# Strips of a banded product in two column tiles, finer weight pieces, and another order of masks, excess strip and first mix groups

## The chip, the cores and the metric

The kernel runs on one core of a Trainium2 chip. The metric is the device time of one launch in microseconds (us), the median of several runs. The engines are TensorE (PE in the profile; its weight loads are PEld), VectorE (DVE), ScalarE (ACT), GpSimd (POOL) and SyncE (SP, which here only issues DMAs). Each engine runs its own queue in order and waits on semaphores.

## The reference

The input x is 4 x 512 rows of 1024 columns, in f32. Two blocks follow each other, and behind each the layer norm of x plus the block's output is taken.

```python
attn = jnp.einsum('ds,td->st', w1, w2) * sparse_mask     # 1024 x 1024
y = jnp.einsum('bds,st->bdt', x, attn) + b2
x = layernorm(x + gelu(y))                               # exact gelu

mask = norm(x, axis=-1) > 64.0
w_l = dequant_kbit(qweight, lut4, 4)                     # 4 bit planes, table of 16 per row
w_h = dequant_kbit(qweight, lut8, 8)
y = jnp.where(mask[..., None], einsum(x, w_h), einsum(x, w_l)) + bias
x = layernorm(x + y)
```

sparse_mask is 1 on windows of 6 along the diagonal and along two more diagonals 32 and 64 beside it, on both sides. So attn is zero outside a band.

## The kernel before, in words

The features are cut into eight units of 128, and the 2048 rows of x into four groups of 512. x is held with features on the partitions, as `z[:, group, unit, 512]`.

**Strips.** Of the product of w1 and w2 only the band is computed, as one strip for each unit b: 128 rows of attn by 272 columns (the unit's own 128 and 72 on each side; 200 columns for the first and the last unit). A strip sums over eight row blocks d of the weights, in f32, each `strip_row(b, d)` being one matmul (two instructions in the trace, L448). `front_strips` makes units 0 to 3, `back_strips(0)` units 4 and 5, `back_strips(1)` units 6 and 7. The weights arrive in pieces: five front pieces, and for each pair of back units two pieces of four row blocks (L285, L286). SP issues them in one queue with the masks of the band, parts of the packed weights and the first pairs of x; that order is the order in which they land.

**Masks.** `mask_strip(b)` on VectorE (L961, L963, L966) multiplies a strip by its mask into mix_raw. ScalarE rounds it to mix_hi (L714) and VectorE subtracts for mix_lo (L973). x is split in the same way, in pairs of units: x_hi on ScalarE (L727) for pairs 1 and 3, on VectorE (L1016) for pairs 0 and 2; x_lo on VectorE (L1018). A few rows of the band reach further than a strip; `excess_strip` (L442) computes them from gathered weights into unit 4's bank, `make_mix_e` (L987 to L999) masks them, and `make_xe_lo` (L1006) makes the matching x.

**Mix.** For each group g, TensorE runs `own(g, t)` (unit t with itself, three matmuls of 512 columns, L481 to L483), `beside(g, t)` (units t and t + 1 with each other, in two row tiles, L506 and L508) and `excess(g, pair)` (L493) into one bank per unit. In group 0 the excess strip stands behind own(0,1), and turn(0) behind own(0,7). ScalarE takes each finished unit through `gelu` (L735), which also frees the bank for the next group. own(g, t) waits for gelu of the group before and for x_lo of its pair; own(1,0) and own(1,1) wait for lin_lo(0) too.

**Decode.** Beside all this, ScalarE and VectorE expand the packed 4-bit weights, block by block (eight blocks), in numbered steps of 11 to a block: a leaf on ScalarE (L753), a merge on VectorE (L1045), two half blocks of planes on VectorE (L1030), a sum of rows and a centring on ScalarE (L758, L763) with the mean between them on VectorE (L1049), and the addition of the identity (L1057). Written lists say how many steps each engine runs at which place: `EARLY_STEPS[b]` ahead of mask b, `MIX_STEPS[g]` in group g (the first number behind gelu(g, 0) and ahead of xe_hi(g + 1), the second further on), `FIRST_STEPS` and `SECOND_STEPS` behind the mix. `turn(b)` on TensorE turns a decoded block, `make_lin_hi` and `make_lin_lo` split it.

**Behind the mix** TensorE multiplies x with the decoded weights, three matmuls of up to 512 columns for each block (L577 to L579), until the end.

Of the kernel before, what the change touches and what calls it, by code (L numbers as in the profile page):

```python
# [38 lines left out]
def post_ln_block(nc, xt, xr, xe_in, w1d, w1e, w2d, w2e, b2c, mask, mask_b, mask_e, mask_rest, qbits, lut4, lut8, bias, out):  # L39
# [26 lines left out]
    HALF_BLOCKS = KB // 2  # L66
    QUARTER = D // 4
# [33 lines left out]
    with ctx:  # L101
# [106 lines left out]
        def by_word(row):  # L208
            return row.rearrange("p (s w k) -> p k s w", s=BITS, k=KB)

        w_loaded = [sem(f"w_loaded{n}") for n in range(len(ROW_PIECES) + 4)]
# [10 lines left out]
        warm_made, consts_made, flips_made = (sem(n) for n in ("warm_made", "consts", "flips"))  # L222
# [7 lines left out]
        ones_made, g_ones_made = sem("ones_made"), sem("g_ones_made")  # L230
# [19 lines left out]
        (g_table_loaded, g_table_step, g_decoded, g_rows_summed, g_row_mean, g_centred, g_w_ready, g_turned, g_lin_hi_made,  # L250
         g_lin_lo,
         g_low_rows, g_bits_made, g_compared, g_blended) = (
             sem(f"g_{n}") for n in ("table", "table_step", "decoded", "rows_summed", "row_mean", "centred", "w_ready", "turned",
# [7 lines left out]

        def places_of(b):
            first, end = strip_of(b)
            return slice(first - b * P + REACH, end - b * P + REACH)
# [7 lines left out]
        def _(sp):  # L272
# [8 lines left out]
            def load_back(n, h):  # L281
                signal = w_loaded[len(ROW_PIECES) + 2 * n + h]
                rows = slice(h * HALF_BLOCKS, (h + 1) * HALF_BLOCKS)
# [148 lines left out]
        def _(pe):  # L432
# [222 lines left out]
            with nc.tensor.If(wanted > 0):  # L655
# [40 lines left out]
                pe.wait_ge(g_ones_made, 1)  # L696
# [6 lines left out]
        def _(act):  # L703
# [37 lines left out]
            def make_leaf(b, i):  # L741
                if i == 0:
# [3 lines left out]
                    if b == 0:  # L746
                        act.wait_ge(flips_made, 1)
# [143 lines left out]
            with nc.scalar.If(wanted > 0):  # L891
# [29 lines left out]
                def general_weights(blocks_before, steps_before, steps):  # L921
                    for h in range(2):
                        with act.Fori(0, HALF_BLOCKS) as c:
# [28 lines left out]
        def _(dve):  # L952
# [56 lines left out]
            def make_x_lo(g, r):  # L1009
                if r in X_ON_ACT:  # L1010
                    dve.wait_ge(x_hi_made, len(X_ON_ACT) * g + X_ON_ACT.index(r) + 1)
                else:
# [4 lines left out]
                    dve.wait_ge(x_rounded, (PAIRS - len(X_ON_ACT)) * g + r // 2 + 1)  # L1017
# [72 lines left out]
            def make_flips():  # L1090
# [11 lines left out]
                                        ALU.subtract).then_inc(flips_made, 1)  # L1102
# [236 lines left out]
            with nc.vector.If(wanted > 0):  # L1339
# [63 lines left out]
                def general_weights(bits, blocks_before, steps_before):  # L1403
                    steps, leaves = table_steps(bits), 2 ** bits
                    for half in range(2):
                        with dve.Fori(0, HALF_BLOCKS) as c:
# [34 lines left out]
                            dve.wait_ge(g_centred, c + (before + 1))  # L1441
# [29 lines left out]
        def _(pool):  # L1471
# [85 lines left out]
            with nc.gpsimd.If(wanted > 0):  # L1557
# [6 lines left out]
                nc.gpsimd.memset(g_ones[:, :].bitcast(f32), 1.0).then_inc(g_ones_made, 1)  # L1564
# [114 lines left out]
```

## Time and profile before

| | |
|---|---|
| median of 3 runs | 296.92 us (295.55 to 296.94) |
| profiled execution | 297.11 us, span 295.1 us |
| TensorE busy | 280.9 us, 95% of the span |
| VectorE busy | 222.3 us, 75% |
| ScalarE busy | 196.1 us, 66% |
| DMA, 7 to 36 us | 374 GB/s |

The span is the time from the first to the last instruction of the profiled execution. Busy shares are means over stages that have different limits; what a hole in one engine costs is read from who waits for it.

### The profile page before, as it was taken

To read this page: it belongs to the slowest core of one execution; us is meant where nothing else is said; L and a number is where in the kernel's file an instruction comes from. 1 tells how busy PE (TensorE), PEld (TensorE's weight loads), DVE (VectorE), ACT (ScalarE), POOL (GpSimd) and SP (SyncE) were. 2 spreads that over 40 slices of the span, in tenths; PEclk is the share of its full clock that TensorE was granted. 3 is DMA by queue.
4 is the path that set the end of the run, shared out by engine and by line. 5 is a ranking of instruction groups with operands and counts; after the bars stand their busy time and mean duration, and the time that the engine had idled before them with its cause. 6 is when DMAs were issued, how large, how long until landed. Compare 5 with 4: busy or idle time off the path is not lost.

```text
span 295.1 us, 4871 instructions
## 1 busy us (share of the span) xinstructions
PE 280.9 (95%) x1835; PEld 245.2 (83%) x1835; DVE 222.3 (75%) x380; ACT 196.1 (66%) x257; POOL 57.0 (19%) x83
## 2 busy tenths in 40 slices
PE   6999999899999999999999999999999999999990
PEld 2788866667668999999999999999988887887780
DVE  1679999897868977997979686297589778656272
ACT  2866368988999879989989996472457484113110
POOL 4000001533354211221200000001141124262101
PEclk9999999999999999999999999999999999999998
DMA  6999999999999711111111111165088754333423
GB/s 207 400 359 359 376 376 340 242 244 244 207 201 195 147 39 36 56 36 51 40 39 53 38 53 38 51 141 221 16 289 273 244 196 178 113 139 117 171 92 132
DMA packets 28480, 49.78 MB, mean 169 GB/s; under 512 B 2464, under 2 KB 11936, under 8 KB 28448
## 3 DMA queue, kind: packets, MB, share of 16 engines
q1 hardware_dynamic: 23392, 40.53, 39.9%
q0 software_dynamic: 4352, 8.39, 15.8%
q10 hardware_dynamic: 704, 0.46, 0.5%
q8 instruction: 17, 0.28, 0.4%
q14 instruction: 15, 0.12, 0.1%
HBM read 36.79 MB, written 12.58 MB: 167 GB/s over the span
## 4 chain that ended last, share of the span: by engine, by line
PE 69%; ACT 7%; SPq 7%; DVE 7%; issue 5%; DMA 3%; POOLq 0%; POOL 0%; DVEq 0%; ACTq 0%
PE acc L577 17%; PE acc L579 17%; PE acc L578 17%; PE acc L506 4%; DMA w<-in_w2d 3%; PE acc L481 2%; SPq L286 2%; ACT leaf L753 2%; ACT zz L796 2%; PE acc L516 2%; PE acc L482 2%; PE acc L483 2%; DVE leaf L1045 1%; PE acc L560 1%; DVE zz L1087 1%
## 5 line engine op out<-in xcount | busy, mean ns | idle before, releaser
L577 PE MATMUL acc<-lin,zz 128*128 128x256 f32 (+2 forms) x424 | 130.7, 308 | 0.3 <-issue 0.3
L579 PE MATMUL acc<-lin,zz 128*128 128x256 f32 (+2 forms) x424 | 129.9, 306 | 0.0
L578 PE MATMUL acc<-lin,zz 128*128 128x256 f32 (+2 forms) x424 | 129.5, 305 | 0.0
L577 PEld LDWEIGHTS acc<-lin,zz 128*128 128x128 f32 x424 | 80.1, 189 | 4.5 <-issue 0.5
L579 PEld LDWEIGHTS acc<-lin,zz 128*128 128x128 f32 x424 | 80.0, 189 | 4.1
L578 PEld LDWEIGHTS acc<-lin,zz 128*128 128x128 f32 x424 | 80.2, 189 | 3.9
L753 ACT ACTIVATE leaf<-planes,lut,flip 128x1024 f32<-128x1024 uint8 x56 | 67.5, 1237 | 1.3 <-DVE dest L1045 1.3
L1045 DVE COPY_PREDICATED leaf<-planes,leaf 128x1024 f32<-128x1024 uint8 x32 | 43.6, 1364 | 13.9 <-ACT leaf L753 13.2
L864 ACT ACTIVATE junk<-rows,cols 128x1024 bf16<-128x1024 f32 x15 | 17.2, 1147 | 34.1 <-DVE cols L1171 34.1
L1045 DVE COPY_PREDICATED dest<-planes,leaf 128x1024 f32<-128x1024 uint8 x24 | 32.5, 1356 | 3.7 <-ACT leaf L753 2.3
L1533 POOL DMA_DIRECT2D z<-in_xr x16 | 19.4, 1218 | 70.9 <-ACT z L735 69.5
L448 PE MATMUL acc<-w,w 128*128 128x272 f32 (+1 forms) x128 | 28.2, 380 | 2.1 <-DMA w<-in_w2d 2.1
L448 PEld LDWEIGHTS acc<-w,w 128*128 128x128 f32 x128 | 23.5, 190 | 7.4 <-DMA w<-in_w2d 3.8
L1165 DVE SCALAR_TENSOR_TENSOR rows<-acc,cols,bias_bc 128x512 f32<-128x512 f32 x15 | 11.3, 750 | 18.4 <-PE acc L579 18.3
L1087 DVE TENSOR_TENSOR zz<-z,zz 128x1024 fp32r<-128x1024 f32 x16 | 19.3, 1220 | 7.6 <-ACT zz L796 7.6
L735 ACT ACTIVATE z<-acc,b 128x512 f32<-128x512 f32 x32 | 20.4, 692 | 4.2 <-PE acc L508 4.2
L846 ACT ACTIVATE parts<-acc 128x258 f32<-128x258 f32 (+1 forms) x32 | 12.1, 379 | 12.8 <-PE acc L579 12.7
L1018 DVE TENSOR_TENSOR x_lo<-z,x_hi 128x1024 fp32r<-128x1024 f32 x16 | 19.0, 1223 | 0.3
L1507 POOL TENSOR_TENSOR cols<-cols 128x4 f32<-128x4 f32 x4 | 5.4, 1352 | 70.3 <-DVE cols L1195 70.3
L1501 POOL TENSOR_SCALAR cols<-parts 128x1 f32<-128x1 f32 x16 | 9.8, 612 | 41.4 <-ACT parts L846 41.4
L796 ACT ACTIVATE zz<-z 128x1024 fp32r<-128x1024 f32 x16 | 16.6, 1064 | 0.0
L851 ACT ACTIVATE off_band<-off_band 128x896 f32<-128x896 f32 x8 | 7.6, 953 | 12.2 <-DMA off_band<-in_mask_rest 12.2
(115 smaller groups left out, 408.4 us busy)
## 6 DMA issues: line engine op xcount, KB each, us to landing
z<-in_xt SPq DMA_DIRECT2D x16, 512.0 KB, 8.7
z<-in_xr POOLq DMA_DIRECT2D x16, 512.0 KB, 8.5
out_rows<-rows SPq DMA_DIRECT2D x15, 512.0 KB, 3.4
out_rows<-parts SPq DMA_DIRECT2D x32, 128.0 KB, 1.7
rows<-out_rows SPq DMA_DIRECT2D x16, 256.0 KB, 2.8
w<-in_w1d SPq DMA_DIRECT2D x7, 512.0 KB, 9.0
off_band<-in_mask_rest SPq DMA_DIRECT2D x8, 448.0 KB, 4.8
w<-in_w2d SPq DMA_DIRECT2D x3, 584.0 KB, 9.0
```

Source lines behind the costliest of these rows:

```text
L448: return nc.tensor.matmul(unit_bank(b)[:, places_of(b)], w1[:, d, b * P:(b + 1) * P], w2[:, d, first:end], start=d == 0, stop=d == KB - 1)
L577: nc.tensor.matmul(bank, hi, w_hi, start=k == 0, stop=False)
L578: nc.tensor.matmul(bank, hi, w_lo, start=False, stop=False)
L579: last = nc.tensor.matmul(bank, lo, w_hi, start=False, stop=k == KB - 1)
L735: nc.scalar.activation(z[:, g, t, :], unit_bank(t), ACT.Gelu, bias=b2[:, t:t + 1]).then_inc(gelu_done, 1)
L753: nc.scalar.activation(to, planes[:, b % 2, 0, :], ACT.Identity, bias=lut[:, b, 2 * i:2 * i + 1], scale=flip[:, b, i:i + 1]).then_inc(leaf ...
L796: nc.scalar.activation(zz[:, 1, g, 2 * r:2 * r + 2, :], z[:, g, 2 * r:2 * r + 2, :], ACT.Copy).then_inc(z_hi_made, 1)
L864: nc.scalar.activation(junk[:, :], rows[:, j % 4, :], ACT.Square, bias=neg_mean2[:, j:j + 1], accum_out=sq2[:, j:j + 1]).then_inc(squared2, 1)
L1018: nc.vector.tensor_tensor(x_lo[:, 2 * r:2 * r + 2, :], z[:, g, 2 * r:2 * r + 2, :], x_hi[:, 2 * r:2 * r + 2, :].bitcast(f32), ALU.subtract ...
L1045: nc.vector.copy_predicated(to, planes[:, b % 2, plane, :], leaf[:, other, :]).then_inc(merged, 1)
L1087: nc.vector.tensor_tensor(zz[:, 0, g, 2 * r:2 * r + 2, :], z[:, g, 2 * r:2 * r + 2, :], zz[:, 1, g, 2 * r:2 * r + 2, :].bitcast(f32), ALU. ...
L1533: nc.gpsimd.dma_start(z[:, g, 2 * r:2 * r + 2, :], xr[g, 2 * r:2 * r + 2].rearrange("k p n -> p k n"), accum_op=ALU.add).then_inc(residual ...
```

## The change

Five things. (1) Each strip row becomes two matmuls: the first 64 rows of the unit with the columns to its left and its own, the last 64 rows with its own and those to its right; each has 64 stationary columns and at most 200 moving ones and writes its own half of the partitions. (2) The back weights come in pieces of two row blocks, four for each pair of units. (3) The excess strip moves behind own(0,3). In group 0 x_hi of pair 0 is made on ScalarE too; mask 6 comes ahead of x_lo(0,1), and mix_hi 6 ahead of x_hi(0,1). (4) In every group beside(g,2) moves ahead of excess(g,0) and beside(g,0); group 1 runs its first four units in the order 2, 3, 0, 1; lin_hi(0) comes behind gelu(0,2). (5) The decode steps are spread anew: 15 instead of 17 early, 5, 4, 4 and 2 in the groups instead of 6, 3, 3 and 2, and one more in the fourth tile behind the mix. The rest joins semaphores of one engine, most of them in a branch that isn't taken with these inputs.

```diff
+    BACK_ROWS = 2
+    BACK_PIECES = KB // BACK_ROWS
...
-    X_ON_ACT = (1, 3)
+    X_ON_ACT = ((0, 1, 3),) + ((1, 3),) * (GROUPS - 1)
...
-    EARLY_STEPS = [11, 1, 1, 1, 1, 2, 0, 0]
-    MIX_STEPS = [(3, 3), (2, 1), (2, 1), (2, 0)]
+    EARLY_STEPS = [13, 1, 1, 0, 0, 0, 0, 0]
+    MIX_STEPS = [(4, 1), (3, 1), (4, 0), (2, 0)]
...
-    FIRST_STEPS = [2, 2, 2, 1, 1, 2, 1, 2, 1, 2, 2, 2, 2, 2, 2, 2]
+    FIRST_STEPS = [2, 2, 2, 2, 1, 2, 1, 2, 1, 2, 2, 2, 2, 2, 2, 2]
...
-    BESIDE = (0, 2, 1, 3, 5, 4, 6)
+    BESIDE = (2, 0, 1, 3, 5, 4, 6)
+    OWN_OF_TURN = (2, 3, 0, 1)
...
             load_back(0, 0)
+            load_back(0, 1)
             load_band(0)
+            load_back(0, 2)
+            load_back(0, 3)
             load_q(1)
-            load_back(0, 1)
             load_back(1, 0)
+            load_back(1, 1)
             load_band(1)
             load_x(0, 0)
-            load_back(1, 1)
+            load_back(1, 2)
+            load_back(1, 3)
             load_x(0, 1)
...
             def strip_row(b, d):
-                first, end = strip_of(b)
-                return nc.tensor.matmul(unit_bank(b)[:, places_of(b)], w1[:, d, b * P:(b + 1) * P], w2[:, d, first:end],
-                                        start=d == 0, stop=d == KB - 1)
+                for rows_, low, high in ((slice(0, SIDE), REACH, 0), (slice(SIDE, P), 0, REACH)):
+                    first, end = max(b * P - low, 0), min((b + 1) * P + high, D)
+                    to = unit_bank(b)[rows_, first - b * P + REACH:end - b * P + REACH]
+                    half = w1[:, d, b * P + rows_.start:b * P + rows_.stop]
+                    last = nc.tensor.matmul(to, half, w2[:, d, first:end], start=d == 0, stop=d == KB - 1)
+                return last
...
             for g in range(GROUPS):
-                for t in range(4):
+                for t in OWN_OF_TURN if g == FIRST_TURN_GROUP + 1 else range(4):
                     own(g, t)
-                    if (g, t) == (0, 1):
+                    if (g, t) == (0, 3):
                         excess_strip()
+                beside(g, 2)
                 excess(g, 0)
                 beside(g, 0)
-                beside(g, 2)
...
                 if b == KB - 1:
-                    make_x_hi(0, 1)
+                    make_x_hi(0, 0)
                 if b:
                     make_mix_hi(b - 1)
+                if b == KB - 1:
+                    make_x_hi(0, 1)
...
                 gelu(g, 1)
                 if g + 1 < GROUPS:
                     make_x_hi(g + 1, 1)
+                gelu(g, 2)
                 if g == FIRST_TURN_GROUP:
                     make_lin_hi(0)
-                gelu(g, 2)
                 gelu(g, 3)
...
                 if b == KB - 2:
                     make_x_lo(0, 0)
+                if b == KB - 1:
                     make_x_lo(0, 1)
                 mask_strip(b)
```

## Rows read from the trace of the kernel before

**Rows 1.** view of stretches; after the length: busy us (and instructions) of each engine, granted clock, DMA
```profile
36.00:63.00 27.00, 24.72 (x152) 17.97 (x151) 24.98 (x37) 20.99 (x27) 5.85 (x7) 1.00 1.04 308
63.00:92.00 29.00, 28.86 (x176) 20.29 (x175) 22.46 (x29) 27.42 (x38) 12.25 (x11) 1.00 1.12 220
92.00:290.00 198.00, 194.79 (x1374) 181.66 (x1372) 149.82 (x252) 126.53 (x170) 35.83 (x54) 1.00 0.35 113
```

**Rows 2.** page, 40 slices: granted clock in tenths
```profile
PEclk9999999999999999999999999999999999999998
```

**Rows 3.** chain of waits, in order of time: start, us, what
```profile
22.22 9.96 DMA w<-in_w2d
32.22 3.45 PE acc L448 x16
```

**Rows 4.** timeline of TensorE: start, us, engine, line, what, idle before
```profile
35.37 0.53 PE L481 MATMUL acc<-x_hi,mix_hi 128*128 128x512 f32 x1
...
36.88 1.88 PE L442 MATMUL acc<-w_e 128*128 128x48 f32 x16
...
41.03 0.39 PE L506 MATMUL acc<-x_hi,mix_hi 64*128 64x512 f32 x1
41.03 0.39 PE L508 MATMUL acc<-x_hi,mix_hi 64*128 64x512 f32 x1
...
44.45 0.47 PE L481 MATMUL acc<-x_hi,mix_hi 128*128 128x512 f32 x1 [0.18 <-DVE x_lo L1018]
...
52.39 0.47 PE L481 MATMUL acc<-x_hi,mix_hi 128*128 128x512 f32 x1 [0.92 <-ACT z L735]
...
57.83 0.47 PE L481 MATMUL acc<-x_hi,mix_hi 128*128 128x512 f32 x1 [0.64 <-DVE x_lo L1018]
```

**Rows 5.** timeline of VectorE, to group 1
```profile
32.05 0.38 DVE L961 TENSOR_TENSOR mix_raw<-acc,band 128x128 f32<-128x128 f32 x1
...
38.80 0.26 DVE L987 TENSOR_TENSOR raw_e<-acc,band_e 128x96 f32<-128x96 f32 x1 [0.42 <-PE acc L442]
...
44.23 1.34 DVE L1045 COPY_PREDICATED dest<-planes,leaf 128x1024 f32<-128x1024 uint8 x1
...
47.40 0.75 DVE L1006 SCALAR_TENSOR_TENSOR xe<-xe_raw,cols,xe 128x512 fp32r<-128x512 f32 x1 [0.28 <-ACT xe L721]
...
48.79 2.36 DVE L1018 TENSOR_TENSOR x_lo<-z,x_hi 128x1024 fp32r<-128x1024 f32 x2
...
68.95 0.63 DVE L1030 TENSOR_SCALAR planes<-q_low 128x256 uint16<-128x256 uint16 x4
```

**Rows 6.** timeline of ScalarE, end of the masks
```profile
32.88 0.42 ACT L714 ACTIVATE mix_hi<-mix_raw 128x256 fp32r<-128x256 f32 x1 [0.61 <-DVE mix_raw L966]
33.49 1.06 ACT L727 ACTIVATE x_hi<-z 128x1024 fp32r<-128x1024 f32 x1 [0.20 <-DMA z<-in_xt]
```

**Rows 7.** timeline of TensorE, groups 2 and 3
```profile
65.31 0.50 PE L481 MATMUL acc<-x_hi,mix_hi 128*128 128x512 f32 x1
...
77.57 0.50 PE L481 MATMUL acc<-x_hi,mix_hi 128*128 128x512 f32 x1
...
82.36 0.50 PE L481 MATMUL acc<-x_hi,mix_hi 128*128 128x512 f32 x1
```

**Rows 8.** timeline of ScalarE, start of group 2
```profile
69.52 0.69 ACT L735 ACTIVATE z<-acc,b 128x512 f32<-128x512 f32 x1 [0.59 <-PE acc L508]
70.11 1.23 ACT L753 ACTIVATE leaf<-planes,lut,flip 128x1024 f32<-128x1024 uint8 x1
71.24 1.14 ACT L763 ACTIVATE dest<-dest,cols 128x1024 f32<-128x1024 f32 x1
72.29 0.61 ACT L721 ACTIVATE xe<-xe_raw 128x512 fp32r<-128x512 f32 x1
```

**Rows 9.** timeline of VectorE, x_lo of group 3
```profile
74.43 2.36 DVE L1018 TENSOR_TENSOR x_lo<-z,x_hi 128x1024 fp32r<-128x1024 f32 x2
...
80.58 2.40 DVE L1018 TENSOR_TENSOR x_lo<-z,x_hi 128x1024 fp32r<-128x1024 f32 x2
```

More of the change, by code:

```diff
@@ L1 @@
+import itertools
 import numpy as np
@@ L81, in post_ln_block @@
     LATE = (LAST_PAIR, LAST_PAIR + 1)
-    X_ON_ACT = (1, 3)
+    X_ON_ACT = ((0, 1, 3),) + ((1, 3),) * (GROUPS - 1)
+    X_HI_BEFORE = list(itertools.accumulate((len(pairs) for pairs in X_ON_ACT), initial=0))
+    X_ROUNDED_BEFORE = [PAIRS * g - n for g, n in enumerate(X_HI_BEFORE)]
     DECODE = LEAVES + 3
-    EARLY_STEPS = [11, 1, 1, 1, 1, 2, 0, 0]
-    MIX_STEPS = [(3, 3), (2, 1), (2, 1), (2, 0)]
+    EARLY_STEPS = [13, 1, 1, 0, 0, 0, 0, 0]
+    MIX_STEPS = [(4, 1), (3, 1), (4, 0), (2, 0)]
     MIX_Z = {2: ((0, 0), (0, 1)), 3: ((0, 2), (0, 3))}
     FIRST_Z = [((1, 0), (1, 1)), ((1, 2),), ((1, 3),)] + [((2 + n // PAIRS, n % PAIRS),) for n in range(2 * PAIRS)] + [()] * 5
-    FIRST_STEPS = [2, 2, 2, 1, 1, 2, 1, 2, 1, 2, 2, 2, 2, 2, 2, 2]
+    FIRST_STEPS = [2, 2, 2, 2, 1, 2, 1, 2, 1, 2, 2, 2, 2, 2, 2, 2]
     SECOND_STEPS = [3, 2, 2, 3, 2, 2, 2, 3, 2, 2, 2, 3, 2, 2, 2, 3]
-    BESIDE = (0, 2, 1, 3, 5, 4, 6)
+    BESIDE = (2, 0, 1, 3, 5, 4, 6)
     HALVES = 2 * len(BESIDE)
     FIRST_TURN_GROUP = 0
+    OWN_OF_TURN = (2, 3, 0, 1)
     TURN_IN_FIRST = {6: 2, 12: 3}
@@ L209, in by_word @@
             return row.rearrange("p (s w k) -> p k s w", s=BITS, k=KB)
-        w_loaded = [sem(f"w_loaded{n}") for n in range(len(ROW_PIECES) + 4)]
+        w_loaded = [sem(f"w_loaded{n}") for n in range(len(ROW_PIECES) + 2 * BACK_PIECES)]
         band_loaded = [sem(f"band_loaded{s}") for s in range(2)]
@@ L221, in post_ln_block @@
         residual_done = [sem(f"residual_done{r}") for r in range(PAIRS)]
-        warm_made, consts_made, flips_made = (sem(n) for n in ("warm_made", "consts", "flips"))
+        warm_made, consts_made = sem("warm_made"), sem("consts")
         planes_made, leaf_made, merged = sem("planes_made"), sem("leaf_made"), sem("merged")
@@ L249, in post_ln_block @@
                                      "x_loaded", "x_hi", "x_lo", "mixed", "gelu", "residual"))
-        (g_table_loaded, g_table_step, g_decoded, g_rows_summed, g_row_mean, g_centred, g_w_ready, g_turned, g_lin_hi_made,
+        (g_table_loaded, g_table_step, g_decoded, g_w_ready, g_turned, g_lin_hi_made,
          g_lin_lo,
          g_low_rows, g_bits_made, g_compared, g_blended) = (
-             sem(f"g_{n}") for n in ("table", "table_step", "decoded", "rows_summed", "row_mean", "centred", "w_ready", "turned",
+             sem(f"g_{n}") for n in ("table", "table_step", "decoded", "w_ready", "turned",
                                      "lin_hi", "lin_lo", "low_rows", "bits", "compared", "blended"))
@@ L260, in strip_of @@
             return max(b * P - REACH, 0), min((b + 1) * P + REACH, D)
-        def places_of(b):
-            first, end = strip_of(b)
-            return slice(first - b * P + REACH, end - b * P + REACH)
         def blocks_of(b):
@@ L281, in load_back @@
             def load_back(n, h):
-                signal = w_loaded[len(ROW_PIECES) + 2 * n + h]
-                rows = slice(h * HALF_BLOCKS, (h + 1) * HALF_BLOCKS)
+                signal = w_loaded[len(ROW_PIECES) + BACK_PIECES * n + h]
+                rows = slice(h * BACK_ROWS, (h + 1) * BACK_ROWS)
                 part, cut = slice(HALF + n * QUARTER, HALF + (n + 1) * QUARTER), slice(turn_of[n], turn_of[n + 1])
@@ L926, in general_weights @@
                             nc.scalar.activation(dest[:, 0, :], dest[:, 0, :], ACT.Copy,
-                                                 accum_out=row_sum[:, 0:1]).then_inc(g_rows_summed, 1)
-                            act.wait_ge(g_row_mean, c + (before + 1))
+                                                 accum_out=row_sum[:, 0:1]).then_inc(rows_summed, 1)
+                            act.wait_ge(row_mean_made, c + (KB + before + 1))
                             nc.scalar.activation(dest[:, 0, :], dest[:, 0, :], ACT.Identity,
-                                                 bias=neg_row_mean[:, 0:1]).then_inc(g_centred, 1)
+                                                 bias=neg_row_mean[:, 0:1]).then_inc(centred, 1)
                             act.wait_ge(g_turned, c + (before + 1))
@@ L1016, in make_x_lo @@
                     nc.vector.tensor_copy(x_hi[:, 2 * r:2 * r + 2, :], z[:, g, 2 * r:2 * r + 2, :]).then_inc(x_rounded, 1)
-                    dve.wait_ge(x_rounded, (PAIRS - len(X_ON_ACT)) * g + r // 2 + 1)
+                    dve.wait_ge(x_rounded, X_ROUNDED_BEFORE[g] + [n for n in range(PAIRS) if n not in X_ON_ACT[g]].index(r) + 1)
                 nc.vector.tensor_tensor(x_lo[:, 2 * r:2 * r + 2, :], z[:, g, 2 * r:2 * r + 2, :],
@@ L1440, in general_weights @@
                                     g_decoded, 1)
-                            dve.wait_ge(g_centred, c + (before + 1))
+                            dve.wait_ge(centred, c + (KB + before + 1))
                             block_ = by_word(dest[:, 0, :])[:, bass.ds(c + HALF_BLOCKS * half, 1), :, :].rearrange(
```

23 lines of the change are left out of this document (11 added, 12 removed).

## The prediction

> **What bounds the kernel now.** I read the stretches first: from 36 to 63 us TensorE is busy 24.72 of 27 us, from 63 to 92 us 28.86 of 29, from 92 to 290 us 194.79 of 198 [rows 1]. So from 63 us on the kernel is a TensorE queue without holes (the holes at the very end are the tail). A microsecond that TensorE wins or loses before 63 us is worth a microsecond at the end, and the only holes that could be won are the 2.3 us between 36 and 63. The granted clock is 1.00 in these stretches [rows 1] and nine tenths or more in all slices but the last [rows 2]: the level of 2.4 GHz. The chain of waits shows what sets the start of the mix: the last weight piece, issued at 22.22, lands at 32.18, and sixteen matmuls follow it [rows 3]. TensorE's timeline shows the rest of the start: own(0,0) at 35.37, the excess strip at 36.88, own(0,6) at 44.45, own(1,0) at 52.39 after 0.92 us idle, own(1,4) at 57.83 after 0.64 us idle for x_lo [rows 4].
>
> **The strips.** The sixteen matmuls behind the last piece are four rows of 272 columns and four of 200, two instructions to a row, in 3.45 us with a tail of about 0.3 us [rows 3]: 0.227 and 0.167 us an instruction, in proportion to the columns, so 0.453 us for a wide row and 0.333 for a narrow one. After the change each row is two halves of 200 moving columns or fewer, and 64 stationary columns. No row of before shows column tiles. If the halves run together, a row costs 0.333 us; if one follows the other, 0.667. Two neighbours: matmuls of two row tiles both start at 41.03 us and both last 0.39 us, so they share their time [rows 4], which speaks for the lower end; the excess strip, with 48 moving columns, takes 1.88 us for sixteen instructions [rows 4], 0.107 for a load and a matmul, and two such pairs for each pass would make 0.43 a row. I take 0.333, because the row pairs are the nearest row, and keep 0.43 and 0.667 for the range.
>
> The Trainium skill, "TensorEngine Tiling (Array Packing)", Key Properties, says that different tiles can load weights and multiply in parallel. By that rule a row would cost what I take; no run here shows it for column tiles. The same list says that a change of the tiling mode drains the engine, which speaks against the change; the strips change mode once, at their end, and the sum would be the same to about a tail.
>
> The weights' bytes and their place ahead of the last piece don't change: the same pieces are halved, and the first x pair and both bands stay ahead of the last one. So it lands at 32.2 as before. Behind it stand two rows of two units instead of four: unit 6 is done after three rows, at 32.2 + 1.0 + about 0.25 = 33.45, unit 7 at 33.8, where the strips now end at 35.67. That is the whole gain of tiles and pieces, 1.9 us; earlier gains only lengthen the waits for the next piece.
>
> **What the masks now hold back.** On VectorE the queue is x_lo(0,0), mask 6, mix_lo 4, x_lo(0,1), mask 7. On ScalarE it is x_hi(0,0), mix_hi 6, x_hi(0,1). Earlier masks are out of the way: mask 5 stands at 32.05 now, in a VectorE that never waits from 21 us on [rows 5]; 15 instead of 17 decode steps lie ahead of it, a merge of 1.34 us and half a block of planes (0.54) less, so it can start by 30.2. With 0.83 for the mask, 0.41 for mix_hi 5, 1.06 for x_hi(0,0) and 1.2 for x_lo(0,0) that pair is made by 33.7 at the latest, and by about 33 if the band's wait of before shrinks. Mask 6 then waits for unit 6: 33.5. A mask takes 0.83 us to its release of mix_hi (32.05 to 32.88) [rows 5, 6], so mix_hi 6 starts at 34.33, takes 0.41, and x_hi(0,1), whose data landed at 33.49, runs from 34.75 for 1.06 us [rows 6]. x_lo(0,1) follows with 1.2 us to 37.05, and own(0,2) starts at 37.2. TensorE has finished own(0,0) and own(0,1) by 35.2: the strips' gain ends in a wait of 2 us.
>
> The excess strip now stands behind own(0,3). From own(0,0) to the excess strip two units took 1.51 us [rows 4]; so it starts at 38.7 in place of 36.88, 1.8 us later, and VectorE, which is in order, starts raw_e at 40.6 instead of 38.80 [rows 5]. Everything behind it in that queue (xe_lo, x_lo(0,2), mix_lo 6 and 7, x_lo(0,3)) keeps its lengths, so own(0,6) starts at 46.25 instead of 44.45. Beside(0,2), moved ahead of excess(0,0), runs in the wait for mix_e and gains nothing, since own(0,4) and own(0,6) wait for x_lo.
>
> **Group 0's decode.** VectorE's first step of the mix moves from 44.23 [rows 5] to 46.05. It is now half a block of planes, about 0.54 us of the 0.63 that one takes [rows 5] since neighbours overlap, and then the mean of block 0. ScalarE's centre waits for this mean until 46.75; behind it in ScalarE's queue stand two leaves, then xe_hi(1): 1.05 + 1.13 + 1.13 + 0.61 (the lengths are those of [rows 8]), so xe_hi(1) ends at 50.7. From the start of xe_lo to the end of the second x_lo it is 3.75 us (47.40 to 48.79 + 2.36) [rows 5], which gives 54.45 and, with 0.15 to TensorE, 54.6. Own(1,2), the first of the new order, needs exactly that x_lo(1,1). Without waits TensorE would be there at 46.25 + 7.0 = 53.25. So group 1 starts at 54.6 against 52.39: +2.2. Starting with units 2 and 3 hides lin_lo(0), which ends 1.15 us behind x_lo(1,1), and with one merge less before x_lo(1,2) the 0.64 us wait at 57.83 goes: -0.6. Group 1's leaves, merges, xe_lo and x_lo(2,0) end 12.2 us after its start, against the 12.26 that a group takes (65.31 to 77.57) [rows 7]: no wait, by a hair. Group 2 starts +1.6 us late.
>
> **Group 2's four steps.** This term doesn't depend on what came before. Now gelu(2,0) starts 4.21 us after own(2,0) (69.52, 65.31), then ScalarE runs a leaf and a centre before xe_hi(3) at 72.29; x_lo(3,0) ends at 74.43 + 1.2 and own(3,0) starts at 77.57 [rows 7 to 9], so it has 1.8 us to spare. Two things eat them. Beside(2,2) and the excess stand ahead of beside(2,0), on whose end gelu(2,0) waits: +0.7 (three passes of 0.23). And four steps come before xe_hi(3) where there were two: one leaf and one sum of rows more, 1.13 + 1.05 = +2.2 [rows 8]. 1.8 - 0.7 - 2.2 = -1.1: group 3 starts 1.1 us late against group 2. In the same way z_hi(0,0), z_lo and x_lo(3,2) come 1.9 us later; x_lo(3,2) ends at 80.58 + 1.2 and own(3,4) starts at 82.36 [rows 7, 9], with 0.4 us to spare behind the 0.15, and the stall gives 1.1 more: 0.4 + 1.1 - 1.9 = -0.4.
>
> **The sum.** 2.2 - 0.6 + 1.1 + 0.4 = +3.1 us on the profiled execution's 297.11, that is 300.2. Its median stands 0.2 below the profiled one, so I forecast 300.0. The decode step moved into the first tiles' turn (a leaf and a merge) goes into idle time of ScalarE or adds up to 0.6 us at the third turn; it stays in the range. Two more edits cost nothing: the joined semaphores, and more DMA issues on SP, which now runs some 9 us ahead of the landings (22.22 against 32.18); that cover gone, four pairs of issues would cost a few us.
>
> **Rivals.** (a) Faster: TensorE alone limits groups 0 and 1. Speaks for it: strips end 1.9 us earlier, a group needs 12.26 us, and the new order takes both named waits out. Groups 0 and 1 from 33.8 with 1.7 us for the excess strip and 1.0 for the turn put group 2 at 61.0 against 65.31, -4.3, and with group 2's +1.5 the time is 294.3. It decides at x_lo(0,1): it would have to be made by 35.2 us, not 37.05. Against it: the orders of both queues. (b) No change that can be told: the decode queues catch up half, group 1 starts less than 0.7 us late: 296 to 298.4. (c) Column tiles one after the other: 5.1 us for each of eight row steps, 6.4 + 40.8, unit 6 near 47 instead of 33.45, +13.5 on top: 313.7. At 0.43 us a row unit 6 is about 1 us later: 301. (d) The clock falls to 1.2 GHz in the new gap of about 2.5 us ahead of the last two pieces. The rows show 1.00 through the waits of before [rows 2], so little speaks for it; the last rows and units would cost twice, some +3: 303.
>
> The Trainium skill, "TensorE: Matmul & The Clock Gate", Part 3, gives 2.38 times for three column tiles of narrow bf16 matmuls. An estimate from that page would put two tiles close to together, so a row near 0.4 us and the result at that of the 0.43 case; nothing here shows it yet.
>
> **How the numbers follow.** Forecast, with 0.333 to 0.43 a row and the uncertainty of each wait (298.4 to 302): 0.64. (a) 0.13, (b) 0.13, (c) with true serial tiles 0.06, (d) 0.04. The range goes from the middle of (b) to (d), 296.9 to 303, and leaves out (a), (c) and a part of (b) and (d). About 0.5% is what a measurement of this kernel can tell from no change: 295.4 to 298.4 is "same". Faster is (a), 0.13; same is (b), 0.13; slower is the rest, 0.74.
>
> **What would show it.** Right: strip halves that start in pairs; unit 7 done near 33.8; own(0,2) idle before it until 37.2, released by x_lo; raw_e near 40.6; own(1,2) near 54.6; own(3,0) idle about 1 us before it. Wrong at once: own(0,2) right behind own(0,1), a last piece that lands much before 32, or own(3,0) without idle time.

## The result, and the profile after

The changed kernel takes 301.11 us (median, 300.32 to 302.02) against 296.63 us of the kernel before: a ratio of 1.0137, with a 95% interval of 1.0112 to 1.0161. Timed again in the run after5 it gave 1.0112 (1.0083 to 1.0141). It is slower: by 4.1 us by the ratio (1.37% of 296.63), by 4.5 us by the two medians; 300.0 was forecast, in a range of 296.9 to 303.0. The profiled execution took 302.02 us with a span of 300.2 us, 5.1 us more than the span before.

First the chain of waits of the changed kernel, in order of time (start, us, what), from the third piece of the last weights to group 1:

```profile
23.77 7.44 DMA w<-in_w2d
31.25 4.29 PE acc L458 x25
...
35.64 0.37 DVE mix_raw L973
...
36.46 0.42 ACT mix_hi L724
36.88 0.96 ACT x_hi L737
...
37.86 1.24 DVE x_lo L1030
...
39.23 0.47 PE acc L491
...
40.84 1.73 PE acc L449 x16
...
42.59 0.27 DVE raw_e L999
...
48.10 0.55 DVE planes L1042 x4
48.65 0.07 DVE cols L1061
...
48.75 1.15 ACT dest L773
49.90 1.18 ACT leaf L763 x2
...
52.07 0.62 ACT xe L731
...
55.25 1.23 DVE x_lo L1030
...
56.62 0.47 PE acc L491
```

It is the chain of the forecast: mask 6 (L973) releases mix_hi 6 (L724), behind it x_hi(0,1) (L737), x_lo(0,1) (L1030), two units of the mix and the excess strip (L449), raw_e (L999); then x_lo(0,3), a plane step, the mean (L1061), the centre (L773), two leaves (L763), xe_hi(1) (L731), and on VectorE the split of x's first two pairs for group 1. What differs from the forecast is its start, 2.1 us late (mask 6 at 35.64 instead of 33.5). TensorE's timeline (the last bracket is the idle time before the instruction and what ended it) has the same places as [rows 4, 7]:

```profile
31.25 4.60 PE L458 MATMUL acc<-w,w 128*64 128x200 f32 x32 [2.10 <-DMA w<-in_w2d]
...
39.23 0.47 PE L491 MATMUL acc<-x_hi,mix_hi 128*128 128x512 f32 x1 [1.78 <-DVE x_lo L1030]
...
40.68 1.88 PE L449 MATMUL acc<-w_e 128*128 128x48 f32 x16
...
48.25 0.47 PE L491 MATMUL acc<-x_hi,mix_hi 128*128 128x512 f32 x1 [0.18 <-DVE x_lo L1030]
...
56.62 0.47 PE L491 MATMUL acc<-x_hi,mix_hi 128*128 128x512 f32 x1 [0.25 <-DVE x_lo L1030]
```

The same timeline from group 2 to own(3,4):

```profile
68.88 0.50 PE L491 MATMUL acc<-x_hi,mix_hi 128*128 128x512 f32 x1
...
82.13 0.47 PE L491 MATMUL acc<-x_hi,mix_hi 128*128 128x512 f32 x1 [0.92 <-ACT z L745]
...
87.40 0.47 PE L491 MATMUL acc<-x_hi,mix_hi 128*128 128x512 f32 x1 [0.47 <-DVE x_lo L1030]
```

| start of, us | before | after | later by |
|---|---|---|---|
| excess strip | 36.88 | 40.68 | 3.8 |
| own(0,6) | 44.45 | 48.25 | 3.8 |
| group 1 | 52.39 | 56.62 | 4.2 |
| group 2 | 65.31 | 68.88 | 3.6 |
| group 3 | 77.57 | 82.13 | 4.6 |
| own(3,4) | 82.36 | 87.40 | 5.0 |

From there on TensorE is nearly without holes, and the 5.0 us arrive at the end. The view of stretches shows it against [rows 1]: the loss is TensorE's idle time between 36 and 63 us, now 4.8 us instead of 2.3, and 1.4 us between 63 and 92, where there was 0.1. In the columns, the figure ahead of the last two is the granted clock:

```profile
36.00:63.00 27.00, 22.16 (x129) 15.77 (x129) 20.77 (x36) 18.48 (x24) 5.17 (x6) 1.00 0.83 265
63.00:92.00 29.00, 27.62 (x168) 19.18 (x166) 24.85 (x32) 26.52 (x36) 10.49 (x9) 1.00 1.12 227
92.00:290.00 198.00, 196.95 (x1385) 182.69 (x1384) 149.20 (x246) 131.89 (x177) 37.48 (x55) 1.00 0.37 113
```

The same view in short stretches, from the strips' last pieces on, with the clock again ahead of the last two figures:

```profile
28.00:29.00 1.00, 1.00 (x14) 0.72 (x10) 0.90 (x4) 0.42 (x1) 0.00 (x0) 1.00 1.12 352
...
30.00:31.00 1.00, 0.00 (x0) 0.00 (x0) 0.95 (x4) 0.40 (x2) 0.00 (x0) 1.00 1.16 358
...
32.00:33.00 1.00, 1.00 (x11) 1.00 (x9) 1.00 (x1) 0.00 (x0) 0.00 (x0) 0.50 1.01 391
...
34.00:35.00 1.00, 1.00 (x10) 0.75 (x9) 0.00 (x0) 0.00 (x0) 0.00 (x0) 0.50 1.05 383
...
36.00:37.00 1.00, 1.00 (x5) 0.82 (x5) 0.84 (x4) 0.54 (x2) 0.00 (x0) 1.00 1.04 379
```

This is what the forecast had only as its rival (d): TensorE has no work from 29.2 to 31.25 us, and soon after the clock stands at 0.50, the level of 1.2 GHz, for over three microseconds. The last thirty-two strip instructions took 4.60 us; at full clock (a_x, below) they take 3.03.

### The profile page after: what moved, and what is told of

The parts are those of the page before. It is cut to its first block, busy times and chain, and to the rows that moved or that the text cites. A ratio compares the mean times of both kernels' runs of the same rounds, so it can differ in the third digit from the quotient of the medians.

```text
span 300.2 us, 5135 instructions
## 1 busy us (share of the span) xinstructions
PE 278.3 (93%) x1963; PEld 242.5 (81%) x1963; DVE 221.4 (74%) x379; ACT 196.3 (65%) x258; POOL 57.2 (19%) x83
## 4 chain that ended last, share of the span: by engine, by line
PE 63%; ACT 10%; DVE 9%; SPq 7%; issue 6%; DMA 2%; POOLq 0%; POOL 0%; ACTq 0%; DVEq 0%
PE acc L587 17%; PE acc L589 16%; PE acc L588 16%; ACT leaf L763 3%; DMA w<-in_w2d 2%; DVE x_lo L1030 2%; SPq L288 2%; ACT zz L806 2%; SPq L289 2%; DVE zz L1099 2%; PE acc L516 2%; PE acc L491 2%; PE acc L526 2%; PE acc L458 1%; PE acc L570 1%
## 5 line engine op out<-in xcount | busy, mean ns | idle before, releaser
L763 ACT ACTIVATE leaf<-planes,lut,flip 128x1024 f32<-128x1024 uint8 x56 | 67.4, 1237 | 1.2 <-DVE dest L1057 0.7
L1546 POOL DMA_DIRECT2D z<-in_xr x16 | 20.2, 1265 | 75.1 <-ACT z L745 70.5
L458 PE MATMUL acc<-w,w 128*64 128x200 f32 (+1 forms) x256 | 25.1, 346 | 5.8 <-DMA w<-in_w2d 5.8
L458 PEld LDWEIGHTS acc<-w,w 128*64 128x64 f32 x256 | 21.0, 144 | 10.1 <-DMA w<-in_w2d 9.0
L1030 DVE TENSOR_TENSOR x_lo<-z,x_hi 128x1024 fp32r<-128x1024 f32 x16 | 19.1, 1223 | 2.2 <-ACT x_hi L737 1.9
L491 PE MATMUL acc<-x_hi,mix_hi 128*128 128x512 f32 x32 | 13.9, 433 | 4.4 <-DVE x_lo L1030 3.4
L1514 POOL TENSOR_SCALAR cols<-parts 128x1 f32<-128x1 f32 x16 | 9.1, 571 | 42.4 <-ACT parts L858 42.4
```

Source lines behind the costliest of these rows:

```text
L458: last = nc.tensor.matmul(to, half, w2[:, d, first:end], start=d == 0, stop=d == KB - 1)
L491: nc.tensor.matmul(bank, hi, x_hi[:, t, :], start=True, stop=False)
L763: nc.scalar.activation(to, planes[:, b % 2, 0, :], ACT.Identity, bias=lut[:, b, 2 * i:2 * i + 1], scale=flip[:, b, i:i + 1]).then_inc(leaf ...
L1030: nc.vector.tensor_tensor(x_lo[:, 2 * r:2 * r + 2, :], z[:, g, 2 * r:2 * r + 2, :], x_hi[:, 2 * r:2 * r + 2, :].bitcast(f32), ALU.subtract ...
L1546: nc.gpsimd.dma_start(z[:, g, 2 * r:2 * r + 2, :], xr[g, 2 * r:2 * r + 2].rearrange("k p n -> p k n"), accum_op=ALU.add).then_inc(residual ...
```

## The experiments

Each run's ratio is to the kernel before on the same chip, with its 95% interval. "Milestones" are starts in the profiled execution, so they are good to some tenths of a microsecond, while the timed runs of one kernel spread over 1 to 3.6 us. A difference of two ratios is shown only where it is larger than their intervals.

**Keep TensorE at work in the wait (a_fill).**

```diff
+                    if n == 1 and d == 2 * BACK_ROWS:
+                        for _ in range(20):
+                            nc.tensor.matmul(unit_bank(KB - 1)[:, 288:512], warm[:, 0:P], warm[:, 0:224], start=False, stop=False)
```

> The changed kernel with twenty bf16 matmuls of 224 columns put into TensorE's wait ahead of the third back piece of units 6 and 7; they write columns that no one reads. Theory (the fallen clock makes the strips late, and each microsecond of strips reaches the end through mask 6, x_hi(0,1) and x_lo(0,1)): the granted clock stays at 1.00, unit 7's strip ends near 34.2 instead of 35.7, own(0,2) starts near 37.7 instead of 39.2, and the time is 299.4 to 300.2. Rival (the end of the strips doesn't matter, the queues behind it do): the strips end earlier, own(0,2) stays at 39.2 and the time at 301.1.

1.0128 (1.0074 to 1.0183), 300.84 us. TensorE's timeline of this run, with the filling matmuls and the last strip instructions:

```profile
29.10 2.09 PE L475 MATMUL acc<-warm 128*128 128x224 bf16 x20
31.23 3.07 PE L458 MATMUL acc<-w,w 128*64 128x200 f32 x32
```

And from own(0,2) to group 1:

```profile
37.69 0.60 PE L494 MATMUL acc<-x_hi,mix_hi 128*128 128x512 f32 x1 [1.80 <-DVE x_lo L1033]
...
40.22 2.39 PE L449 MATMUL acc<-w_e 128*128 128x48 f32 x16
...
56.66 0.47 PE L494 MATMUL acc<-x_hi,mix_hi 128*128 128x512 f32 x1 [0.28 <-DVE x_lo L1033]
```

The first half came as expected. The strips end at 34.3 and own(0,2) starts at 37.69, so the strips' end does set it, and the rival falls. But no time is won: the wait for x_lo(0,1) is still 1.80 us, and now the clock falls there. It stood at 0.50 from 37.9 to 41.3 us; the excess strip took 2.39 us instead of 1.88, raw_e starts at 42.65 as without the filling (42.59), and group 1 at 56.66. The clock fell once more, from 44.7 to 48.1 us. That one cost the chain nothing: from own(0,4) to group 1 it is 10.16 us, and 10.17 in the changed kernel, whose clock was full there.

**One matmul a row again (a_wide).**

```diff
-                for rows_, low, high in ((slice(0, SIDE), REACH, 0), (slice(SIDE, P), 0, REACH)):
-                    ...
+                first, end = strip_of(b)
+                to = unit_bank(b)[:, first - b * P + REACH:end - b * P + REACH]
+                return nc.tensor.matmul(to, w1[:, d, b * P:(b + 1) * P], w2[:, d, first:end], start=d == 0, stop=d == KB - 1)
```

> The changed kernel with each strip row again as one matmul of up to 272 columns; two-row pieces and all orders stay. Theory (two column tiles only turn strip time into waits for the weights, and let the clock fall): TensorE has no hole over 1 us before the last piece, the clock stays at 1.00, the strips end near 34.9, own(0,2) starts near 38.4, and the time is 300.5 to 301.3, not worse than with the tiles. Rival (the tiles' shorter rows are a gain of their own): the strips end 0.5 us or more later than 35.7 and the time is 301.8 to 303.

1.0178 (1.0135 to 1.022), 302.15 us; the profiled execution took 301.62. TensorE's timeline of this run, the strips and then own(0,2):

```profile
10.82 24.25 PE L456 MATMUL acc<-w,w 128*128 128x200 f32 x112 [0.85 <-DMA w<-in_w2d]
...
38.44 0.47 PE L488 MATMUL acc<-x_hi,mix_hi 128*128 128x512 f32 x1 [1.98 <-DVE x_lo L1027]
```

The profile has what the theory said: the strips run without a hole, the clock stays at 1.00 past the mix, the strips end at 35.07, own(0,2) starts at 38.44 and group 1 at 55.83, 0.8 us earlier than in the changed kernel's profile. So up to the mix the tiles are no gain when the clock falls in the strips; when it holds (a_fill, a_x), their strips end at 34.3, 0.8 us ahead of a_wide's. The timed runs don't show these 0.8 us: the interval overlaps that of the changed kernel and lies, if anything, above it, though in the profile most of the lead is still there at the last turn (200.36 against 201.02). Why stays open.

**x's second pair ahead of mask 6 (a_x).**

```diff
                 if b == KB - 1:
                     make_x_hi(0, 0)
+                    make_x_hi(0, 1)
                 if b:
                     make_mix_hi(b - 1)
-                if b == KB - 1:
-                    make_x_hi(0, 1)
...
                     make_x_lo(0, 0)
-                if b == KB - 1:
                     make_x_lo(0, 1)
```

> The changed kernel with x_hi(0,1) ahead of mix_hi 6 on ScalarE and x_lo(0,1) ahead of mask 6 on VectorE. Theory (mask 6 ahead of x's second pair costs TensorE a wait of 1.8 us ahead of own(0,2) and so moves the excess strip): own(0,2) follows own(0,1) without idle time, raw_e starts near 40.6 instead of 42.6, group 1 near 54.6, and the time is 2 us less than the changed kernel's, 298.7 to 299.5. Rival (mask 6 and 7 come later and their mix_lo hold back own(0,4) to own(0,6) just as much): 300.6 to 301.4.

1.0076 (1.0046 to 1.0105), 299.60 us: 1.5 to 1.8 us won against the changed kernel, just short of the 2 us expected. The wait ahead of own(0,2) is 0.51 us instead of none, the excess strip starts at 37.83 instead of 40.68, group 1 at 53.77. That is 2.85 us in the profile, of which 1.6 are the strips' end at 34.26 with the clock at 1.00. In this execution it fell only at 43.9 us, which again cost the chain nothing: the last turn comes 2.80 us earlier, too. What the order alone is worth is read against a_g2 (below), which has the changed kernel's order up to group 2 and nearly the same history of the clock: the excess strip starts 1.36 us earlier here (37.83 against 39.19), group 1 1.35 us (53.77 against 55.12). TensorE's timeline of this run at own(0,2):

```profile
36.37 0.47 PE L491 MATMUL acc<-x_hi,mix_hi 128*128 128x512 f32 x1 [0.51 <-DVE x_lo L1029]
```

**And the excess strip behind own(0,1) (a_x_exc).**

```diff
-                    if (g, t) == (0, 3):
+                    if (g, t) == (0, 1):
```

> The changed kernel with x's second pair ahead of mask 6 (as in the run before with that edit alone) and the excess strip back behind own(0,1). Theory (raw_e and all behind it on VectorE wait for the excess strip): raw_e starts near 38.4 instead of 39.75 of that run, group 1 1.3 us earlier, and the time is 1.0 to 1.5 us less than with x's pair alone, a ratio to the kernel before of 1.002 to 1.005. Rival (mask 7 and mix_lo 5 to 7 set raw_e or own(0,4) by then): the same ratio as with x's pair alone, 1.0076.

1.0045 (1.0024 to 1.0065), 298.55 us, another 0.9 us in the ratio, inside what was expected; the interval overlaps that of a_x, so by time alone the step isn't shown. The profile has it: group 1 starts at 52.94, 0.8 us earlier than in a_x, although the clock fell again behind the wait ahead of the last pieces and the strips ended 1.3 us later, at 35.58.

**Two of group 2's steps moved to group 3 (a_g2).**

```diff
-    MIX_STEPS = [(4, 1), (3, 1), (4, 0), (2, 0)]
+    MIX_STEPS = [(4, 1), (3, 1), (2, 0), (4, 0)]
```

> The changed kernel with two of group 2's four decode steps moved to group 3: MIX_STEPS of (4,1), (3,1), (2,0), (4,0). Theory (the leaf and the sum of rows ahead of xe_hi(3) make group 3 late, whatever came before): own(3,0) starts 12.3 us after own(2,0) instead of 13.25 and own(3,4) 4.8 us after own(3,0) instead of 5.3, 1.4 us won; group 3's longer list then delays z_hi and z_lo of the pairs that the first squares wait for, by up to 1.3 us, so the time falls by 0 to 1.2 us against the changed kernel. Rival (group 3 waits for something that these steps don't move): own(3,0) stays 13.2 us behind own(2,0).

Group 3 starts 12.29 us after group 2 (79.64, 67.35), and own(3,4) 4.78 us after that: the mechanism is as it was read. No time is won, 1.0164 (1.0119 to 1.021), where 0 to 1.2 us were expected: the steps in group 3 now keep z_lo back, and the first squares wait for it, as TensorE's timeline of this run shows:

```profile
94.80 2.17 PE L570 MATMUL acc<-zz 128*128 128x256 f32 x16 [1.72 <-DVE zz L1099]
```

Up to group 2 this is the changed kernel, and in its profile the clock held until about 43 us. So it shows that kernel's start of the mix at full clock. TensorE's timeline has the excess strip, VectorE's has mask 6:

```profile
39.19 1.88 PE L449 MATMUL acc<-w_e 128*128 128x48 f32 x16
```

```profile
34.13 0.38 DVE L973 TENSOR_TENSOR mix_raw<-acc,band 128x128 f32<-128x128 f32 x1 [0.72 <-PE acc L458]
```

**The same two steps taken to the place ahead of mask 6 (a_early).**

```diff
-    EARLY_STEPS = [13, 1, 1, 0, 0, 0, 0, 0]
-    MIX_STEPS = [(4, 1), (3, 1), (4, 0), (2, 0)]
+    EARLY_STEPS = [13, 1, 1, 0, 0, 0, 2, 0]
+    MIX_STEPS = [(4, 1), (3, 1), (2, 0), (2, 0)]
```

> The changed kernel with two of group 2's steps taken to the place ahead of mask 6, where VectorE waits: EARLY_STEPS of 13, 1, 1, 0, 0, 0, 2, 0 and MIX_STEPS of (4,1), (3,1), (2,0), (2,0). Theory (the mean of block 0 first in group 0 keeps ScalarE's centre, xe_hi(1) and group 1 waiting; two steps too many do the same in group 2): own(0,2) stays where it is, xe_hi(1) comes 1.1 us earlier against own(0,6), group 3 starts 12.3 us after group 2, and the time is 2.0 to 2.8 us less than the changed kernel's. Rival (the steps ahead of mask 6 delay x_lo(0,0) and mask 6 by what they save later): no gain beyond 0.5 us.

1.0121 (1.0088 to 1.0153), 300.80 us: the timed runs can't tell it from the changed kernel (1.0137 and 1.0112), and the expected 2.0 to 2.8 us were too much. In the profile the later parts come as expected: group 3 follows group 2 by 12.24 us, without a wait behind it, and nothing waits at the squares. From own(0,6) to group 1 it is 7.97 us instead of 8.37, 0.4 us won where 1.1 was expected: the leaf behind the second one needs a merged buffer, and ScalarE waits for VectorE's merge. But the rival is right in part. The clock held in this execution, and the strips ended at 34.28, yet mask 6 starts only at 35.39, as VectorE's timeline shows:

```profile
34.14 1.23 DVE L1030 TENSOR_TENSOR x_lo<-z,x_hi 128x1024 fp32r<-128x1024 f32 x1 [1.22 <-ACT x_hi L737]
35.39 0.38 DVE L973 TENSOR_TENSOR mix_raw<-acc,band 128x128 f32<-128x128 f32 x1
```

The two steps keep x_hi(0,0) on ScalarE back to 33.06 (30.93 in the changed kernel), and with it x_lo(0,0) and mask 6. Against a_g2, whose strips end at 34.34, mask 6 and the excess strip are 1.3 us late (35.39 against 34.13, 40.46 against 39.19). So at full clock these steps cost 1.3 us ahead of the mix, of some 1.9 us that they win behind it (0.4, 1.0 and 0.5 at groups 1 and 3 and own(3,4)). In the changed kernel's own profile, with the fallen clock, VectorE waits 2.42 us ahead of mask 6, so there was room for them.

**All three orders undone (a_sum).** The edits of a_x, a_x_exc and a_early together.

> The changed kernel with its three order parts undone together: x's second pair ahead of mask 6, the excess strip behind own(0,1), and the step lists of 13, 1, 1, 0, 0, 0, 2, 0 and (4,1), (3,1), (2,0), (2,0). Tiles, two-row pieces, beside(g,2) first and group 1's new order stay. Theory (the orders explain the loss; their parts add up): group 1 starts near 52.5, group 3 near 77.1, the ratio to the kernel before is 0.998 to 1.003. Rival (tiles and pieces cost by themselves, through the clock or late landings): 1.005 or more.

0.9974 (0.9957 to 0.9992), 296.66 us, just below the expected range. The orders were the loss: undone together they win 1.4% against the changed kernel timed beside it (1.0112) and end a little below the kernel before, with the tiles still there and the clock still falling for three microseconds ahead of the strips' end. Group 1 starts at 53.41 and group 3 at 77.93, 0.9 and 0.8 us later than expected. One by one the edits gave 0.61%, 0.31% and 0.16% in the ratios, 1.1% in all, each with some 0.3% to either side, so they add up to the 1.4% no better than within that; the last two aren't shown singly by the times.

**Only tiles and two-row pieces (b_tiles), only tiles (b_tiles4).** The kernel before with the change's strip_row and loads, every order as before; and with strip_row alone.

```diff
-                return nc.tensor.matmul(to, w1[:, d, b * P:(b + 1) * P], w2[:, d, first:end], start=d == 0, stop=d == KB - 1)
+                for rows_, low, high in ((slice(0, SIDE), REACH, 0), (slice(SIDE, P), 0, REACH)):
+                    ...
```

> The kernel before with only the two column tiles and the two-row pieces; every order and every list of steps as before. Theory (in the old order VectorE's two x_lo and masks 6 and 7, not the strips, set the start of raw_e): raw_e stays within 0.5 us of 38.8 and the time is that of before, 296.1 to 297.1. Rival (the shorter strips reach the end): own(0,0) near 34, raw_e near 37.2 and 294.8 to 295.4.

> The kernel before with the two column tiles alone; the weights in four-row pieces as before. Theory (in the run with two-row pieces in the old order it was band 0, landing 1 us late behind more and smaller transfers, that moved the masks): the first mask starts at 20.5 again, raw_e within 0.3 us of 38.8, the ratio is 0.999 to 1.001 as long as the clock holds; if it falls in the wait of some 2.5 us ahead of the last piece, eight rows at half the clock end the strips near 37.5 and the ratio is 1.004 to 1.007. Rival (the tiles, not the pieces, moved the masks): the first mask starts near 21.5 again.

b_tiles: 1.0052 (1.003 to 1.0075), 298.36 us; b_tiles4: 1.001 (0.9988 to 1.0032), 297.46 us. Neither theory holds; in b_tiles4 the rival does (the tiles, not the pieces, moved the masks). In both, the tiles win nothing: the strips end at 35.8 and 35.5 us (35.67 before), and the first mask starts at 21.5 and 21.4 us, where the kernel before has 20.5 and the two profiles of the next kernel, which has no tiles, 21.07 (b_own) and 20.40 (b_own5). VectorE waits for the band's mask to land (L964 and L962 are the mask's line in either kernel). VectorE's timeline at that mask, first of b_tiles4:

```profile
21.43 0.39 DVE L964 TENSOR_TENSOR mix_raw<-acc,band 128x128 f32<-128x128 f32 x1 [1.48 <-DMA band<-in_mask_b]
```

And of b_own5, which has no tiles:

```profile
20.40 0.38 DVE L962 TENSOR_TENSOR mix_raw<-acc,band 128x128 f32<-128x128 f32 x1 [0.85 <-DMA band<-in_mask_b]
```

Everything behind is late by this: raw_e starts at 39.71 and 39.73 instead of 38.80 (39.35 and 38.60 in b_own and b_own5). Part of this is spread: in b_own the landings up to the first band are 0.6 us later than in the kernel before, in b_tiles4 0.4 us already at the last front piece. Counted from there, the first band transfer lands after 4.0 us in the profiles without tiles and after 4.5 in b_tiles4, 5.3 in b_tiles. The pieces alone are not the cause, since b_tiles4 has four-row pieces and a_wide, with two-row pieces, has 4.0; nor is the clock, which never fell in b_tiles4 up to the mix's end. What differs is the width of the strips' matmuls. A clean pair are the changed kernel and a_wide, which issue the same band transfer at the same 11.6 us; the time to its landing follows, first in the changed kernel, with tiles:

```profile
L293 SPq DMA_DIRECT2D band<-in_mask_b x1: 1387/1387/1387, 11.6 to 11.6; - x1
...
DMA to landing us min/median/max: 9.8/9.8/9.8
```

And in a_wide, without them:

```profile
L293 SPq DMA_DIRECT2D band<-in_mask_b x1: 1378/1378/1378, 11.6 to 11.6; - x1
...
DMA to landing us min/median/max: 9.0/9.0/9.0
```

**Only group 1's new order (b_own, b_own5).** The kernel before with the parts of the change that act on group 1.

```diff
-    MIX_STEPS = [(3, 3), (2, 1), (2, 1), (2, 0)]
+    MIX_STEPS = [(3, 2), (2, 2), (2, 1), (2, 0)]
+    OWN_OF_TURN = (2, 3, 0, 1)
...
-                for t in range(4):
+                for t in OWN_OF_TURN if g == FIRST_TURN_GROUP + 1 else range(4):
...
+                gelu(g, 2)
                 if g == FIRST_TURN_GROUP:
                     make_lin_hi(0)
-                gelu(g, 2)
```

> The kernel before with only group 1's order 2, 3, 0, 1, lin_hi(0) behind gelu(0,2), and one step moved from group 0 to group 1: MIX_STEPS of (3,2), (2,2), (2,1), (2,0). Theory (the parts of the change that take waits out of group 1 are a gain when nothing else is moved): the 0.92 us wait ahead of group 1 and the 0.64 us ahead of own(1,4) go, group 2 starts 1.0 to 1.5 us earlier than 65.3, and the ratio to the kernel before is 0.994 to 0.997. Rival (the waits only move, to x_lo of group 1 or 2): 1.000.

> The kernel of b_own again, to have its interval: the kernel before with group 1's order 2, 3, 0, 1, lin_hi(0) behind gelu(0,2), and one step moved from group 0 to group 1. By its first run: a ratio of 0.992 to 0.995, and no wait of TensorE on VectorE or ScalarE between 46 us and the end of the mix. A rival (its first run had a lucky clock): 0.997 to 1.000.

0.9931 (0.9907 to 0.9955) and 0.9936 (0.992 to 0.9952), 295.05 and 295.56 us: faster than both kernels. The edit is three things at once (the order of units, lin_hi(0), one step moved from group 0 to group 1); they were not tried apart. The waits of TensorE between 46 and 92 us are gone from the list of who waited for whom; what is left is issue time behind the mix. The view of TensorE's waits of b_own5, 46 to 92 us:

```profile
PE acc L578 <- issue: 0.3, 1, 0.3
```

Group 2 starts 19.24 us after own(0,6) (63.50, 44.26) where it was 20.86 [rows 4, 7]: 1.6 us, the 0.92 and the 0.64 of the two waits.

**The changed kernel again (after5).**

> The changed kernel itself, on the same chip as the others of this call: by its record a ratio of 1.011 to 1.016 to the kernel before, own(0,2) behind a wait of 1.8 us for x_lo, and group 3 13.25 us behind group 2; the clock falls for some 3 us in one of the waits between 28 and 43 us, not always in the same.

1.0112 (1.0083 to 1.0141). The wait ahead of own(0,2) is 1.79 us, group 3 follows group 2 by 13.27 us. The clock fell twice, from 31.0 to 34.4 us and from 44.7 to 48.1 us; from own(0,4) to group 1 it is 10.17 us all the same.

The budget from the ratios: group 1's new order -0.67% (mean of b_own and b_own5), tiles and two-row pieces +0.52% (b_tiles), the three orders +1.38% (1.0112 against 0.9974). Together +1.23%, where the changed kernel measured +1.37% and +1.12%. The last term is itself taken from the 1.0112, so what the sum really tests is a_sum: the first two terms give -0.15%, and it measured -0.26% (-0.43 to -0.08). x_hi of pair 0 on ScalarE, beside(g,2) first and the step added behind the mix stay in a_sum and were not tried alone.

## Why the prediction was right

The forecast of 3.1 us came as 4.1 by the ratio, 4.5 by the medians and 5.1 in the spans of the profiled executions. The delays behind the strips came by the steps it named and in nearly their sizes; what is too small in the sum is the strips' term, and it alone accounts for the difference in the profile: own(0,6) is 2.0 us later than forecast, group 1 2.0, own(3,4) still 1.9.

- **The strips.** Column tiles do run together: a_x has thirty-two instructions, eight rows, in 3.03 us with the tail, so 0.34 to 0.35 us a row at full clock, where 0.333 was taken; so the rivals of 0.43 and 0.667 a row fell. The end at 33.8 was not reached: the earliest of any run is 34.26. This is the mis-sized term. The last piece landed at 32.6 instead of 32.2 (0.4 us; 32.2 in a_wide, without tiles). And the clock fell behind the wait ahead of the last two pieces, which was priced as rival (d) at "some +3" with a chance of 0.04. It fell there in five of the nine profiles that have this wait of 2.0 to 2.1 us, at 1.5 to 1.6 us each. Unit 6 was done at 35.6 instead of 33.45. The reason given against (d), a clock of 1.00 through the waits of before, was weak: no wait of TensorE ahead of the mix was longer there than 1.08 us. That the time still lies in the range, whose upper end is that of (d), is in part luck.
- **What the masks hold back.** From unit 6 to own(0,2) it was forecast as 3.75 us and took 3.6 (35.64 to 39.23). The wait of 1.78 us and the later excess strip came as said, own(0,6) 3.8 us late: 1.8 of the order, by the forecast, and 2.0 of the strips' term. a_g2 separates the two. There the clock held until about 43 us, and mask 6 starts at 34.13 for 33.5 forecast, the excess strip at 39.19 for 38.7, raw_e at 41.10 for 40.6, group 1 at 55.12 for 54.6: the forecast's times, each 0.5 to 0.6 us late. That much of the strips' term is landing and row price, and 1.5 us is the clock. a_x and a_x_exc undo the order.
- **Group 0's decode.** From own(0,6) to group 1: 8.37 us, forecast 8.35. Both named waits of group 1 went, -0.66 against -0.6.
- **Group 2's four steps.** Group 3 started 0.99 us late against group 2 (forecast 1.1), own(3,4) another 0.48 (forecast 0.4). ScalarE's timeline, against [rows 8], has the leaf and the sum of rows (L768 with its read) that were added ahead of xe_hi(3) at 78.71:

```profile
73.78 0.69 ACT L745 ACTIVATE z<-acc,b 128x512 f32<-128x512 f32 x1 [1.52 <-PE acc L518]
74.37 1.23 ACT L763 ACTIVATE leaf<-planes,lut,flip 128x1024 f32<-128x1024 uint8 x1
75.50 1.05 ACT L768 ACTIVATE dest<-dest 128x1024 f32<-128x1024 f32 x1
76.45 0.19 ACT L768 ACTIVATION_READ_ACCUMULATOR dest<-dest 128x1 f32 x1
76.54 1.23 ACT L763 ACTIVATE leaf<-planes,lut,flip 128x1024 f32<-128x1024 uint8 x1
77.67 1.14 ACT L773 ACTIVATE dest<-dest,cols 128x1024 f32<-128x1024 f32 x1
78.71 0.62 ACT L731 ACTIVATE xe<-xe_raw 128x512 fp32r<-128x512 f32 x1
```

x_lo(3,0) is done at 80.76 + 1.22 us, just ahead of 82.13. The profile names a gelu as what ended that wait, but own(3,0) waits only for gelu(2,0), which had ended at 74.5.

- **The rival of the other side** (TensorE alone limits groups 0 and 1) fell where the forecast said that it would be decided, at x_lo(0,1), made at 39.1 us instead of by 35.2. The part of it that was right is group 1's new order: alone it is worth 1.6 us in the profile and about 2 us by the ratios.

Open are a_wide's timed runs, and how column tiles delay a transfer.

## What to carry to other kernels

When a faster stage ends in a wait for the same transfer, look at what stands in the other engines' queues behind its last result: here one mask ahead of one pair of x, and the excess strip two units later, made that strip start 2.3 us late though the strips before it ended 1.3 us early (a_g2 against the kernel before). A list of background steps has to be read against the one product that the next stage waits for (here xe_hi of the next group), since two steps more ahead of it cost 1 us wherever else the engine idles. And a change of five parts should be tried part by part: group 1's new order gained 0.67% by itself, while the whole lost 1.1 to 1.4%. Ahead of a new wait, the clock belongs in the range with more than a few per cent, if no row shows a wait as long.

## What the runs showed of the hardware

The clock can fall behind a wait of 2 us between dense stretches of matmuls. In the nine profiles with a wait of 2.0 to 2.1 us ahead of the last pieces it fell to 0.50 within 1.1 us behind it in five (the changed kernel twice, a_x_exc, a_sum, b_tiles) and not in four (a_x, a_g2, a_early, b_tiles4). In a_x and a_g2 it fell at 43 to 44 us instead, behind waits of 0.8 to 1.0 us, and in after5 and a_fill a second time at 44.7. In a_fill it also fell behind a wait of 1.80 us, and in a_wide it did not behind one of 1.98. In the kernel before, b_own and b_own5, where TensorE has no wait over 1.3 us, it was full up to the end of the mix. Each fall lasted a little over 3 us. So it is a risk, not a certainty. What a fall costs depends on the place: 1.5 to 1.6 us in the strips (4.60 against 3.03 us), and nothing at 44 us, where TensorE waits for VectorE anyway (10.17 us from own(0,4) to group 1 with the fall and without).

Column tiles of f32 matmuls ran together: two halves of 64 stationary and up to 200 moving columns took 0.34 to 0.35 us a row, where one after the other would take 0.667 by the forecast's working from the columns.

Matmuls in two column tiles went along with later landings. From the last front piece to the landing of the first band transfer it took 4.0 us in the four profiles without tiles (the kernel before, b_own, b_own5, a_wide) and 4.5 to 5.5 us in the ten with tiles, with the same bytes and the same order up to there. The runs don't show by which path.
